# A four-layer graph network on one core: key terms as one row per part, layers 1 and 2 interleaved, selectors made later, last batch finished graph by graph

## What is computed

```python
# layer 0: relational convolution; with adj in {0, 1} only the loop relation counts
h = x @ W.T;  vals = (h + b) * sigmoid(h @ Wg.T + bg)
out = relu((adj_t == 1) @ vals)
# layer 1: attention with a full bilinear term, one head
e = where(adj > 0, leaky_relu(Ax.T + Ay + (h @ a_12) @ h.T), -9e15)
out = elu(x @ W_1 + (softmax(e) @ x) @ W_2)
# layer 2: multi-head attention, 8 heads of 16, masked by adj
out = softmax(where(adj, q @ k.T / 4, -inf)) @ v @ Wo.T + bo
# layer 3: graph attention, 8 heads: e[h,i,j] = e1[h,i] + e2[h,j]
e = leaky_relu(where(adj, e1[:, :, :, None] + e2[:, :, None, :], -inf))
out = softmax(e) @ Wh
```

## Time and profile before

| | |
|---|---|
| median of 3 runs | 698.7 us (698.46 to 699.27) |
| profiled execution | 700.79 us |
| its span in the trace | 699.1 us |
| PE busy | 629.2 us, 90% |
| DVE / ACT / POOL busy | 569.5 (81%) / 524.4 (75%) / 513.1 us (73%) |
| loads | nearly all in the first two of 40 slices of 17.5 us |

### The profile page before, as it was taken

One profiled execution on the slowest core, in us unless ns is written; L12 is line 12 of the kernel. 1 busy time (PEld: TensorE's weight loads), 2 busy tenths in 40 slices (PEclk: granted clock), 3 DMA queues, 4 the chain that ended last, 5 costly groups with the idle time before them and its releaser, 6 DMA issues.

```text
span 699.1 us, 17607 instructions
## 1 busy us (share of the span) xinstructions
PE 629.2 (90%) x5948; PEld 461.5 (66%) x5994; DVE 569.5 (81%) x2442; ACT 524.4 (75%) x823; POOL 513.1 (73%) x542
## 2 busy tenths in 40 slices
PE   3999799999779999999999999879999998999972
PEld 2888677777456666676666666657676676766652
DVE  5799759999578888888888888679888888788862
ACT  2554389999558777777777776668999989899882
POOL 6377628999595567777777766758887788777884
PEclk9999899999779999999999999999999999999997
DMA  9900000000200000000000000000000001000011
GB/s 254 288 10 1 1 1 1 2 1 0 91 1 1 1 3 2 1 2 1 2 1 2 2 2 1 3 3 4 7 29 19 19 18 30 22 17 19 19 32 46
DMA packets 31302, 16.80 MB, mean 24 GB/s; under 512 B 3558, under 2 KB 30444, under 8 KB 31212
## 3 DMA queue, kind: packets, MB, share of 16 engines
q1 hardware_dynamic: 27744, 14.46, 7.8%
q10 hardware_dynamic: 3468, 1.20, 0.8%
HBM read 9.59 MB, written 4.19 MB: 20 GB/s over the span
## 4 chain that ended last, share of the span: by engine, by line
PE 53%; DVE 17%; SPq 10%; issue 5%; POOL 5%; ACT 4%; DMA 4%; DVEq 1%; ACTq 0%; POOLq 0%
PE pair L1121 17%; SPq L532 10%; PE pair L1312 5%; PE quad L1261 4%; DMA mask<-eT 4%; DVE arena L1026 3%; PE quad L1174 3%; PE pair L1277 2%; PE pair L1283 2%; PE pair L1193 2%; PE quad L1164 2%; PE pair L1291 2%; DVE bn L580 2%; PE quad L1185 2%; PE pair L1185 2%
## 5 line engine op out<-in xcount | busy, mean ns | idle before, releaser
L669 POOL TENSOR_TENSOR arena<-arena,nmx 128x1024 f32<-128x1024 f32 x64 | 121.3, 1895 | 68.3 <-DVE nmx L1052 68.3
L1121 PE MATMUL pair<-identf,arena 128*128 128x128 f32 x880 | 122.7, 281 | 0.0
L555 POOL TENSOR_SCALAR X<-yb,ln 128x128 f32<-128x128 f32 x256 | 113.7, 456 | 5.1
L1121 PEld LDWEIGHTS pair<-identf,arena 128*128 128x128 f32 x880 | 95.1, 142 | 25.8 <-issue 25.8
L691 POOL TENSOR_TENSOR arena<-arena,nmx 128x1024 f32<-128x1024 f32 x38 | 72.1, 1897 | 32.2 <-DVE nmx L1026 32.1
L548 POOL TENSOR_TENSOR ln<-ln,neghalf 128x4 f32<-128x4 f32 x64 | 66.9, 1046 | 32.9 <-DVE ln L589 32.7
L817 ACT ACTIVATE arena<-quad 128x1024 f32<-128x1024 f32 x64 | 65.9, 1030 | 27.7 <-PE quad L1215 17.7
L1043 DVE TENSOR_TENSOR arena<-quad,mask 128x1024 f32<-128x1024 f32 x64 | 77.8, 1215 | 3.6 <-PE quad L1261 3.0
L1052 DVE TENSOR_REDUCE nmx<-arena 128x8 f32<-128x1024 f32 x64 | 78.1, 1220 | 1.8
L867 ACT ACTIVATE arena<-arena 128x1024 f32<-128x1024 f32 x64 | 68.1, 1064 | 1.1 <-POOL arena L669 1.1
L580 DVE BATCH_NORM_STATS2 bn<-yb 128x6 f32<-128x128 f32 x256 | 58.3, 279 | 11.5 <-POOL yb L698 9.6
(11 more groups left out here) (200 smaller groups left out, 1498.3 us busy)
## 6 DMA issues: line engine op xcount, KB each, us to landing
X<-in_x SPq DMA_DIRECT2D x16, 256.0 KB, 5.5
arena<-in_adj SPq DMA_DIRECT2D x16, 256.0 KB, 5.5
out<-X SPq DMA_DIRECT2D x16, 256.0 KB, 2.3
mask<-eT SPq DMA_DIRECT2D x128, 2.2 KB
mask<-sel SPq DMA_DIRECT2D x6, 256.0 KB
nat_all<-in_L_gnn_W ACTq DMA_DIRECT2D x2, 64.0 KB, 5.3
w<-in_L_gnn_W ACTq DMA_DIRECT2D x2, 64.0 KB, 6.1
nat_all<-in_L_gnn_W_loop ACTq DMA_DIRECT2D x1, 64.0 KB, 3.0
```

The lines of the kernel that those rows point to most:

```text
L555: last = nc.gpsimd.tensor_scalar(x_of(b)[:, cols(g)], y_of(L, b)[:, cols(g)], ln[s][:, g:g + 1], ln[s][:, G + g:G + g + 1], ALU.add, ALU.mult)
L669: nc.gpsimd.tensor_tensor(v3(P2[t % 3], HEADS), v3(P2[t % 3], HEADS), nmx2[t % 2][:].unsqueeze(2).broadcast_to([128, HEADS, N]), ALU.add)\
L1121: last = nc.tensor.transpose(dst[:, cols(i)], src[:, cols(i)], identf[:])
```

## The change

It has these parts. (1) The fills of `sel1` and `sel2` leave POOL's start and become one instruction in each of eight steps of layer 2 (`SELECTOR_STEPS`), ahead of that step's less_max; SP's six copies of `sel1` into `mask1` wait for them (`POOL_SET`), and lay the columns out by head, then graph. (2) DVE clears `vx` before the bias split. (3) On PE, layer 0's transposes of batch b + 1 go ahead of the products of batch b. (4) Loads of batches 8 to 15 count x and adj on one semaphore. (5) `enter` replaces the four steps `layer2(-4..-1)` and reorders the last steps of layer 1 with the first of layer 2 on every engine; keys and queries of batch 0 are made in `layer1(16)`. (6) `terms(b)` issues three transfers, one for each part: 8 partitions x 768 bytes into a single row, 32 part + 16, which `eT` multiplies by a one. (7) The last batch of layer 3 is summed, gets its statistics (DVE) and is normalised (POOL) graph by graph, in the groups 0 to 2 and 3, and is stored in two transfers.

```diff
+SELECTOR_STEPS = (5, 7, 8, 9, 11, 12, 13, 17)
+POOL_SET = 17
+LEFT, ENTERED = (2, 4), 5
-def later_layers(layer1, layer2, layer3):
+def later_layers(layer1, enter, layer2, layer3):
     for t in range(BATCHES + 1):
         layer1(t)
-    for t in range(-4, 0):
+    enter()
+    for t in range(1, ENTERED):
         layer2(t)
-    for t in range(3):
-        layer1(BATCHES + 1 + t)
-        layer2(t)
+        if t in LEFT:
+            layer1(BATCHES + 2 + LEFT.index(t))
     two_layers(layer2, layer3)
...
         def first_q(b):
-            return bank[5] if b < 0 else bank[7]
+            return bank[2] if b < 0 else bank[7]
...
-            sp.wait_ge(sem("pool_ready"), 1)
+            sp.wait_ge(sem("pool_set"), POOL_SET)
             sp.wait_ge(sem("L1_logits_mm"), BATCHES)
             for i in range(2 * (G - 1)):
-                sp.dma_start(mask1[:, bass.ts(i, HEADS * N)], sel1[:]).then_inc(sem("L3_terms"), 16)
+                sp.dma_start(graphs_of(i // (G - 1))[:, i % (G - 1)], v3(sel1[:], HEADS)).then_inc(sem("L3_terms"), 16)
...
-                for h in range(HEADS):
-                    to = terms_of(b)[2 * HEADS + h:2 * HEADS + h + 65:32, :].rearrange("p (g c) -> p g c", g=G - 1)
-                    sp.dma_start(to[:, :, cols(h)], eT[b % 2][h:h + 65:32, D:].rearrange("p (g c) -> p g c", g=G - 1))
+                for part in range(3):
+                    row = 32 * part + 2 * HEADS
+                    sp.dma_start(terms_of(b)[row:row + 1, :].rearrange("p (h c) -> p h c", h=HEADS),
+                                 eT[b % 2][32 * part:32 * part + HEADS, D:]).then_inc(sem("L3_terms"), 16)
...
 POOL
+            def enter():
+                norm_pool(pool, 1, BATCHES - 3, (BATCHES - 3) % 2, 0)
+                layer2(0)
+                residual(BATCHES - 2)
+            def layer2(t):
+                if t in SELECTOR_STEPS:
+                    selectors(SELECTOR_STEPS.index(t))
...
+            def last_graphs(k, end):
+                b, s = BATCHES - 1, (BATCHES - 1) % 2
+                rstd = ln[s][:, G:2 * G]
+                pool.wait_ge(sem("last_stats"), end)
+                nc.gpsimd.tensor_tensor(rstd[:, k:end], rstd[:, k:end], neghalf[:, k:end], ALU.pow).then_inc(sem("rstd"), 1)
+                pool.wait_ge(sem("rstd"), LAYERS * BATCHES - 1 + (2 if k else 1))
+                for i in range(k, end):
+                    last = nc.gpsimd.tensor_scalar(x_of(b)[:, cols(i)], y_of(3, b)[:, cols(i)], ln[s][:, i:i + 1],
+                                                   rstd[:, i:i + 1], ALU.add, ALU.mult)
+                last.then_inc(sem("last_norm"), 1)
...
+                if t == GRAPHS + 5:
+                    last_graphs(0, G - 1)
+                if t == GRAPHS + 6:
+                    last_graphs(G - 1, G)
 ACT
+            def enter():
+                exponential(BATCHES - 1)
+                keys_out(0)
+                queries_out(0)
+                transposed_out(BATCHES - 1)
+                negative(BATCHES - 2)
+                negative_exp(BATCHES - 2)
+                layer2(0)
 DVE
+            for s in range(2):
+                nc.vector.memset(vx[s][:], 0.0).then_inc(sem("dve_set"), 1)
...
+            def enter():
+                stats_dve(dve, 1, BATCHES - 3, (BATCHES - 3) % 2)
+                layer2(0)
+                elu_sum(BATCHES - 2)
+                normalised(BATCHES - 1)
...
+            def last_graphs(k):
+                b, s = BATCHES - 1, (BATCHES - 1) % 2
+                y, m = y_of(3, b)[:, cols(k)], mv[s][:, 3 * k:3 * k + 3]
+                if k == 0:
+                    dve.wait_ge(sem("L3_norm_done"), BATCHES - 2)
+                dve.wait_ge(sem("L3_on"), GRAPHS - G + k + 1)
+                nc.vector.tensor_tensor(y, y, x_of(b)[:, cols(k)], ALU.add).then_inc(sem("last_y"), 1)
+                dve.wait_ge(sem("last_y"), k + 1)
+                nc.vector.bn_stats(bn[s][:, cols(k, 6)], y)
+                dve.drain()
+                nc.vector.bn_aggr(m[:, 0:2], bn[s][:, cols(k, 6)])
+                dve.drain()
+                nc.vector.tensor_reduce(ln[s][:, k:k + 1], m[:, 0:1], AX.X, ALU.add, negate=True)
+                nc.vector.tensor_reduce(ln[s][:, G + k:G + k + 1], m[:, 1:3], AX.X, ALU.add).then_inc(sem("last_stats"), 1)
 PE
             def layer0(b, s, turn):
+                if real(b + 1):
+                    pe.wait_ge(*loaded("x", b + 1))
+                    need(pe, sem("L0_xT"), b + 1)
+                    transposes(bank[0], x_of(b + 1), G).then_inc(sem("L0_xT_mm"), 1)
                 if real(b):
...
+                if t == BATCHES:
+                    pe.wait_ge(sem("L2_xT"), 1)
+                    mm(first_k(-1), kT_w[:], xT[0][:], start=True, stop=True).then_inc(sem("L2_k_mm"), 1)
+                    pe.wait_ge(sem("L1_leaky"), BATCHES)
+                    mm(first_q(-1), qT_w[:], xT[0][:], start=True, stop=True).then_inc(sem("L2_q_mm"), 1)
+            def enter():
+                turn_p(BATCHES - 1)
+                pe.wait_ge(sem("L1_xw"), BATCHES)
+                layer2(0)
+                aggregate(BATCHES - 1)
...
                 if j == 1 and real(b):
+                    if b == 0:
+                        pe.wait_ge(sem("L1_z"), BATCHES)
```

More of the change, by code:

```diff
@@ L103, in sem, with loaded @@
             return sems[name]
+        def loaded(what, b):
+            return (sem(f"{what}_loaded{b}"), 16) if b < BATCHES // 2 else (sem(f"loaded{b}"), 32)
         quad = ctx.enter_context(nc.psum_tensor("quad", [128, 2048], F32))
@@ L626, in _ @@
             select(headmask[:], [[HD, HEADS]], HD - 1, ALU.is_ge, 0.0, -1)
-            for part in range(3):
-                select(sel2[:].rearrange("p (h c) -> p h c", h=HEADS), [[-1, HEADS], [0, 128]], -32 * part)
-                select(sel1[:].rearrange("p (h c) -> p h c", h=HEADS), [[-1, HEADS], [0, 128]], -32 * part - HEADS)
             select(center[:], [[0, 128]], 1 - D, fill=-1.0)
@@ L761, in _, with exponential, negative @@
             general_act(act, read_flag(act))
+            def exponential(b):
+                act.wait_ge(sem("L1_less_max"), b + 1)
+                need(act, sem("L1_pT_mm"), b - 1)
+                nc.scalar.activation(e1[b % 2][:], lk[b % 2], ACT.Exp).then_inc(sem("L1_exp"), 1)
+            def negative(b):
+                act.wait_ge(sem("L1_z"), b + 1)
+                need(act, sem("L1_y_done"), b - 1)
+                nc.scalar.activation(elu[b % 2][:], z1[b % 2][:], ACT.Relu, bias=minus_one[:], scale=-1.0).then_inc(sem("L1_neg"), 1)
@@ new lines, in negative_exp, with transposed_out, queries_in @@
+            def negative_exp(b):
+                act.wait_ge(sem("L1_neg"), b + 1)
+                nc.scalar.activation(elu[b % 2][:], elu[b % 2][:], ACT.Exp, scale=-1.0).then_inc(sem("L1_elu_exp"), 1)
+            def transposed_out(b):
+                act.wait_ge(sem("L1_pT_mm"), b + 1)
+                need(act, sem("L1_z_mm"), b - 1)
+                nc.scalar.copy(pT1[b % 2], bank[4]).then_inc(sem("L1_pT"), 1)
+            def queries_in(b):
+                act.wait_ge(sem("L2_xT_mm"), b + 1)
+                if b == 0:
+                    act.wait_ge(sem("L1_xw_mm"), BATCHES - 1)
+                elif b == 1:
+                    act.wait_ge(sem("L1_xw_mm"), BATCHES)
+                else:
+                    act.wait_ge(sem("L2_v_mm"), b - 1)
+                nc.scalar.copy(xT[b % 2][:], proj(G * (b - 1))).then_inc(sem("L2_xT"), 1)
@@ new lines, in keys_out @@
+            def keys_out(b):
+                act.wait_ge(sem("L2_k_mm"), b + 1)
+                need(act, sem("L2_s_mm"), G * (b - 1))
+                if b == 0:
+                    act.wait_ge(sem("kmask_set"), 2)
+                    act.wait_ge(sem("mask2_made"), BATCHES)
+                k = kk[b % 2].rearrange("p (g e n) -> p e g n", g=G, e=2)
+                for e in range(2):
+                    last = nc.scalar.activation(k[:, e], v3(first_k(b - 1), G), ACT.Identity, bias=bk2[:, e:e + 1],
+                                                scale=evenodd[:, e:e + 1])
+                last.then_inc(sem("L2_k"), 1)
@@ new lines, in queries_out @@
+            def queries_out(b):
+                act.wait_ge(sem("L2_q_mm"), b + 1)
+                need(act, sem("L2_s_mm"), G * (b - 1))
+                nc.scalar.activation(qT[b % 2], first_q(b - 1), ACT.Identity, bias=qk_bias[:, 2:3],
+                                     scale=HD ** -0.5).then_inc(sem("L2_q"), 1)
+            def enter():
[6 more added lines that the diff above has]
+                layer2(0)
```

193 lines of the change are left out of this document (101 added, 92 removed).

## The result

The changed kernel takes 679.64 us (median; 679.33 to 682.0) beside 698.71 for the kernel before: a ratio of 0.972, with a 95% interval of 0.9692 to 0.9748. That is 19.1 us less. The profiled execution took 679.49, with a span of 677.8; the profiled one of before had a span of 699.1, so the traces differ by 21.3. 2.1 of it is that the profiled execution of before lay above its median.

The account below looks back on a forecast made before the run. Stages bind differently: DVE in layer 0, POOL's list at the entry, ACT hiding layer 3's wait. Start 4.0 + entry 7.0 + key terms 0.5 + 0 + tail 3.0 = 14.5 us off 698.7: 684.2; own range 679 to 688.2, 8-in-10 range 677 to 690.

Parts of the forecast that it names:

- Start: Start to layer 0: bias split without POOL's selects, and PE's new order, save 4.0 us (bounds 0.5 and 4.6).
- Selectors in layer 2: Layer 2, POOL: two fills and six selects are hidden in the 3.6 us steps, except at steps 5 and 7.
- threat of up to 8.8 us in layer 2: Layer 2: selects could hold up DVE through the shared port, up to 8 times 1.1 us, where DVE isn't the bound.
- selector at step 5: Layer 2, POOL still catching up: a selector there costs 0 to 1 us, 0.5 taken off the entry's gain.
- Entry: Layer 1 to layer 2: the new order shortens POOL's list, 7.0 us saved (9.3 full clock, 5.0 half clock up to 202).
- Key terms: Layer 3: three issues instead of eight save 0.5 us in the first batch, 0 in the others (bounds 0 and 8.2).
- Tail: End of layer 3: finishing the last batch graph by graph saves 3.0 us (bounds 2.5 and 3.3).
- Rival D: Layer 3: single-row transfers land much later, scores(1) of every batch waits; slower, about 715 at 7 us landing; chance 0.04.
- Rival E: Layer 3: three issues take as long as eight did, so 684.7 us; counted with the forecast.

Follow-up runs that it names:

- after: The changed kernel with all parts of the change, against the kernel before: 679.64 us, ratio 0.972.
- entry_only: The kernel before with only layers 1 and 2 interleaved (enter and the steps behind it): 691.77 us, ratio 0.9869.
- twelve_pieces: The changed kernel with the same bytes of key terms in twelve issues of two heads each: 702.91 us, ratio 1.0052 to the kernel before.
- after_again: The changed kernel measured again, beside the kernel before on one chip: 680.7 us, ratio 0.9717.
- exit_later: The changed kernel with later selector steps, and layer 1's last two steps behind steps 3 and 5 of layer 2: 678.25 us, ratio 0.9704 to the kernel before.
- tail_only: The kernel before with only the last batch finished graph by graph and loads counted on fewer semaphores: 696.11 us, ratio 0.9933.
- terms_only: The kernel before with only the key terms moved in three issues per batch instead of eight: 697.82 us, ratio 0.9954.

## Why the prediction was right

The forecast was 684.2, within 677 to 690; measured were 679.6. The sum of 14.5 should have been 18.5, and 0.6 more isn't assigned. Only the start was too large, by 0.2; all other terms were too small, and the gain of 19.1 lies just below the 19.7 that the bounds allowed. Term by term:

- **Start, 4.0: right, 3.8** (2.9 and, less certain, 0.8). The split behaves as worked out: 0.29 for each cast, 2.8 us from the first cast to PE's first product (forecast 2.8). DVE gets 2.9 of the 3.4, because PE's first products and transposes still run at 1.2 GHz then, and PE's order gives 0.8 instead of 0.5. The long casts are named rightly: the row of 1.02 us lies beside the selects, and all casts are short without them, in every trace. The Trainium skill ("SBUF — State Buffer", section "SBUF: two separate sides") explains it by an exclusive lock of DVE and GpSimd on one port pair. The traces agree at the start: what begins while a select of 1.09 us runs ends 0.1 to 0.3 us behind that select (see the last section).
- **Selectors in layer 2, 0: right.** The prediction read the same section as a threat of up to 8.8 us in layer 2, and that was read too widely: the section names DVE's two-port modes, and instructions with two SBUF inputs, as those that take the pair. The mask addition there has PSUM as one input, and 64 of them take 1204 to 1225 ns whether one select runs, two or none. The 0.5 us for the selector at step 5 was 0.
- **Entry, 7.0: 8.1.** The order and the place of the bound (POOL's list) were right: graph 0's scores begin at 174.55, where 181.5 minus the 4.3 of the start and the 2.5 of the crossing gives 174.7. The step that failed is the price of the clock. The forecast had 9.3 with PE at full clock throughout and took off 1.8, since PE would run at half clock until about 192 behind a wait of 2.5 us. PE does wait 2.31 us ahead of 179.71. In after it keeps 1.00; in entry_only and twelve_pieces it doesn't, and the entry is as short (37.78 and 37.80), because POOL's list ends no later. So those 1.8 us are 0; a later fall, in after_again, costs 1.25. The other error goes the other way: 9.3 at full clock were 8.1. The difference is the norm work ahead of the maxima on POOL, of which exit_later takes 1.1 away. The two partly cancel, and that the term came within 1.1 us is luck to that extent.
- **Key terms, 0.5 and 0: 2.4.** The mechanism was right (a batch isn't 0.63 us shorter), the size wasn't. In the first batch it was 0.3 instead of 0.5. The last batch was left out: it has no copy of xT ahead of the slope, so the wait shows, 0.5 us. And the hidden wait wasn't hidden everywhere: up to 0.2 us in some batches and 1.1 in one, where the issues are slower. A wait of 0.50, of which ACT hides about 0.45 (the slope comes 0.06 later), was called zero; it had no margin, and each irregularity of the queue came through. The profile before had it: "8.2, 13, 1.6" in the earlier trace rows says that the longest of the thirteen waits was 1.6.
- **Tail, 3.0: 4.2.** The pow was priced at 1.02, that of four columns. For one column it takes 0.55, for three 0.85. And the landing was left as it was (2.79 us from the last scale to the end) though the last store is a quarter in size: 2.05. Both were within reach, as it was said that the stores are smaller.
- **Rival D** (slower by single-row transfers) didn't come near: there are about 3.5 us of slack (by an estimate: the last issue begins near 572.0 in after, the terms are in 1.7 later, and PE asks for them at 577.3). Its "in at 579.3" counts the last issue twice: in the earlier trace rows the landing of 1.73 begins with that issue, at 576.96, so they were in at 578.7. Twelve pieces show its mechanism, at 1.2 us a batch. **Rival E** is out, three issues take 2.0 us.
- **Not foreseen:** the crossing from layer 0 to layer 1 is 2.5 us longer in some executions. This is most of why the traces differ by 21.3 and the medians by 19.1.

## What to carry to other kernels

Measure stages between fixed marks of the timeline: here layers 1 and 2 repeat to 0.15 us where whole executions differ by 2 to 4, the start, the crossing and the entry show where an execution differs, and one trace of each part alone was enough to assign 18.5 of the 19.1 to 20.0 us. Look at the clock and at the stage together: half the clock on an engine that isn't the bound there cost nothing. A wait that is hidden by a few tenths is not free: look at the longest of its occurrences, not at the mean, and at the batches where the cover is missing. Price a small instruction by its own number of columns, and let the engine with the longest list do first what others wait for.

## What the hardware showed that was not expected

- DVE's steps of the bias split end only behind the select of POOL that runs when they begin. Casts and copies take 1.02 to 1.20 us beside the selects instead of 0.28 or 0.29, but the first cast takes 0.29 where a select ends within 0.15 us of its start (tail_only and terms_only). The fp32 subtraction, with two inputs in SBUF, is no exception: 0.40 where it begins between two selects (and the next select is then the long one, 1.28 instead of 1.09), 0.56 beside a short one of 0.29, 1.36 beside a whole one. Before, then tail_only, where a select runs from 11.40 for 1.09 us:

```profile
8.78 1.19 DVE L931 COPY bias<-bias_part 1x512 bf16<-1x512 bf16 x1
9.90 0.40 DVE L933 TENSOR_TENSOR bias_rest<-bias_rest,bias_part 128x256 f32<-128x256 f32 x1
```

```profile
11.41 1.36 DVE L957 TENSOR_TENSOR bias_rest<-bias_rest,bias_part 128x256 f32<-128x256 f32 x1
```

- POOL is held up by DVE too. In after the maximum that begins at 177.89 takes 2.27 us instead of 1.90 and the pow at 187.60 takes 1.46 instead of 1.02, each beside DVE's ELU sum (L1089, two inputs in SBUF). Every other maximum and pow of layer 2 in this trace is free of that sum and takes the shorter time. What the first costs no run shows; the second costs nothing, since in entry_only the pow takes 1.02 and the entry is as long.

```profile
177.72 0.68 DVE L1089 SCALAR_TENSOR_TENSOR elu<-z,elu 128x512 f32<-128x512 f32 x1
187.39 0.80 DVE L1089 SCALAR_TENSOR_TENSOR elu<-z,elu 128x512 f32<-128x512 f32 x1 [1.43 <-ACT elu L826]
```

- The granted clock at one place of one program differs between executions (1.00 or 0.50 in the crossing, 1.00 or 0.72 in the entry). Behind the same 2.3 us without a matmul in the entry it stays at 1.00 in after and falls in entry_only and twelve_pieces.
- An issue of a transfer on SP costs 0.745 us for three partitions of three pieces, and 0.60 to 0.67 into a single row: the shape counts beside the number.
- GpSimd's pow: 0.55 us for one column, 0.85 for three, 1.02 for four.
